# Feed-forward finish: the order of VectorE's maxima, scales and the second quarter's outputs

## The chip, the cores and the metric

The kernel runs on one core of one Trainium2 chip. The metric is the time of one execution in microseconds (us), as the device reports it. It was timed three times before the change: 2646.08, 2651.69 and 2651.78 us, median 2651.69 us.

The engines are named here as the profile names them: PE is TensorE, DVE is VectorE, ACT is ScalarE, POOL is GpSimd, SP is SyncE with the DMA queue. Each engine takes its instructions in program order; they meet only at semaphores.

## The reference

A decoder of six residual blocks for four batches of 1024 tokens of width 512. Only the last block is touched:

```python
x = _layernorm(x + _L1_xattn_ref(x, ctx_1024, ctx_1024), axis=-1)
x = _layernorm(x + _L1_ffn_ref(x, w1, conv_w, conv_b, w2), axis=-1)

def _L1_ffn_ref(...):                      # hidden width 2048
    h = bit_linear(x, w1)                  # quantised rows of x, ternary weights
    h = depthwise_conv1d(h)                # three taps along the tokens
    h = jax.nn.silu(h)
    return bit_linear(h, w2)

def act_quant(x):
    scale = 127.0 / jnp.clip(jnp.max(jnp.abs(x), axis=-1, keepdims=True), 1e-05)
    return jnp.clip(jnp.round(x * scale), -128, 127) / scale
```

So the second product needs, for every token, the largest absolute value over all 2048 hidden channels before any channel can be rounded. That maximum is what the change is about.

## The kernel before

`schedule(b)` writes out by hand, for each batch, one list of steps. Every engine walks the same list and does its own share of each step, so the list is the program order of all five engines at once.

The feed-forward takes the tokens of a batch in four quarters of 256 (`NSUB` is 4, s is 0 to 3; "the second quarter" is s = 1), and the hidden channels in 16 chunks of 128 (`M`), two chunks to a pair (k or i is 0 to 7). The steps, with the lines on which they show in the profile:

- `f_hidden(s, m)`: PE multiplies one chunk (L750). DVE takes it out of PSUM (f_g, L1357) and adds the last tap of the chunk two before (`last_tap`, L1089). ACT does the middle and first taps (L982, L984) and, with every second chunk, the SiLU of a pair (L808). POOL adds the first tap (L1418). `f_tail` is the rest of that pipeline after the last chunk: two taps on DVE, the SiLU of the last two pairs on ACT, two sums on POOL.
- `f_peak(s, k)`: PE transposes the pair (L759), DVE takes the maxima of it (f_top, L1367). At the last pair DVE goes on to the scales: five small operations (L1373 to L1377) and two diagonals (L1380).
- `f_scale(s)`: PE spreads the scales over the partitions (L765), ACT copies them to f_s2b (L992).
- `f_times(s, i)`: a pair of SiLU outputs times the scales (L374). POOL does it for all pairs of quarters 0 and 1 and pairs 0 to 4 of quarter 2; DVE does the rest.
- `f_quant(s, k)`: ACT rounds four chunks to f_hq (L1002).
- `f_part(s, t, k)`: PE multiplies four chunks by w2 into bank 6 or 7 (L778; before the first four a constant, L775). The first one of each output tile waits until the bank's previous output has been read.
- `f_out(s, t)`: DVE reads that bank and adds the residual (L1388), then two statistics (L1032, L1033); POOL makes the reciprocal deviation (rstd, L1405 and L1407).
- `f_norm(s, t)`: DVE normalises the tile (L1038), SP stores both tiles of a quarter.

Hidden chunks, `f_peak` and a few others share a ring of three PSUM banks (`dve_ring`): PE may claim the next bank only when DVE has emptied the one three claims before.

The twelve projections that open the next batch's attention (`a_key`, `a_query`, `a_value`) are spread among the chunks. The last of them is `a_key(3)`: eight records of matmul on PE (L386) and one copy on ACT (L839). The fourth batch has none.

The order after the last chunk comes from offsets: a step with offset n of quarter s stands behind chunk 16(s+1)+n of the 64, and whatever is past 63 stands after `f_tail`, in order of that number. The steps of the last quarter's maxima have offsets capped so that they come early. Before the change the list around the last chunk of a batch reads:

```
62: f_hidden(3,14) f_times(2,2) f_quant(2,0)
63: f_hidden(3,15) f_part(1,0,3) f_peak(3,3)
f_tail
64: f_out(1,0) f_part(1,1,3) f_times(2,3) a_key(3) of the next batch
65: f_out(1,1) f_peak(3,4) f_peak(3,5)
66: f_times(2,4) f_quant(2,1) f_peak(3,6) f_peak(3,7)
67: f_norm(1,0) f_part(2,0,0)
68: f_norm(1,1) f_times(2,5) f_part(2,1,0)
70: f_times(2,6) f_quant(2,2)
71: f_part(2,0,1)     72: f_times(2,7) f_part(2,1,1)
73: f_scale(3)        74: f_quant(2,3) f_times(3,0) to f_times(3,3)
```

and then the parts and outputs of quarters 2 and 3. The next batch's attention begins when they are done.

Of the kernel before, what the change touches and what calls it, by code (L numbers as in the profile page):

```python
# [30 lines left out]
M = F // P  # L31
# [42 lines left out]
def attends_until(i):  # L74
# [4 lines left out]
FIRST_PROJECTIONS = [("a_key", 0), ("a_query", 0), ("a_value", 0), ("a_key", 1), ("a_value", 1), ("a_query", 2),  # L79
                     ("a_value", 2), ("a_query", 1), ("a_value", 3), ("a_key", 2), ("a_query", 3), ("a_key", 3)]  # L80
# [72 lines left out]
def schedule(b):  # L153

    steps = (WARM_UP if b == 0 else []) + [("a_begin",), ("weight", 3)]
    for i in range(len(GROUPS) + 2):
        g, k = divmod(i, 5)
# [67 lines left out]
    at = {}  # L225
    for s in range(NSUB):
        last = s == NSUB - 1
        later = [(min(2 * k + 9 - M, k // 2 - 1) if last else 2 * k + 9 - M, ("f_peak", s, k)) for k in range(M // 2)]
        later += [(9 if last else 10, ("f_scale", s)),
                  (32, ("f_out", s, 0)), (33, ("f_out", s, 1)), (35, ("f_norm", s, 0)), (36, ("f_norm", s, 1))]  # L230
        later += [((10 if i < 4 else 18) if last else 10 + 2 * i, ("f_times", s, i)) for i in range(M // 2)]
        later += [(14 + 4 * k, ("f_quant", s, k)) for k in range(4)]
        later += [(19 + 4 * k + t, ("f_part", s, t, k)) for k in range(4) for t in range(2)]
        for offset, step in later:
            at.setdefault(M * (s + 1) + offset, []).append(step)
# [2 lines left out]
                    (10, ("f_unit", 1))):  # L238
        at.setdefault(n, []).append(step)
    if b < B - 1:  # L240
        for n, step in zip((2, 3, 5, 6, 14, 21, 28, 35, 42, 49, 56, 64), FIRST_PROJECTIONS):
            at.setdefault(n, []).append(("next", step))
    for n in range(NSUB * M):
        steps += [("f_hidden", *divmod(n, M))] + at.pop(n, [])
# [36 lines left out]
def sequence(nc, dram, sb, banks, sems):  # L281

    order = [step for b in range(B) for step in schedule(b)]
    q = sems
    now = [0]
# [1459 lines left out]
```

## Time and profile before

| | us |
|---|---|
| median of three runs (lowest, highest) | 2651.69 (2646.08, 2651.78) |
| the profiled execution's own time | 2647.19 |
| its span, first to last instruction | 2645.4 |
| PE busy (89% of the span) | 2362.2 |
| DVE busy (60%) | 1578.6 |
| ACT busy (47%) | 1243.5 |
| POOL busy (26%) | 687.5 |
| mean granted TensorE clock | 0.975 |

All times of the trace are read against the 2645.4 us span. Between span and time lie 1.8 us. The four batches are alike; the end of the third batch's feed-forward lies at about 1970 to 2003 us, that of the fourth at 2610 to 2642 us. The busy shares are averages over stages with different limits, so a change in the order of one stage is read from the timeline of that stage.

### The profile page before, as it was taken

To read this page: it belongs to the slowest core of one execution; us is meant where nothing else is said; L and a number is where in the kernel's file an instruction comes from. 1 tells how busy PE (TensorE), PEld (TensorE's weight loads), DVE (VectorE), ACT (ScalarE), POOL (GpSimd) and SP (SyncE) were. 2 spreads that over 40 slices of the span, in tenths; PEclk is the share of its full clock that TensorE was granted. 3 is DMA by queue.
4 is the path that set the end of the run, shared out by engine and by line. 5 is a ranking of instruction groups with operands and counts; after the bars stand their busy time and mean duration, and the time that the engine had idled before them with its cause. 6 is when DMAs were issued, how large, how long until landed. Compare 5 with 4: busy or idle time off the path is not lost.

```text
span 2645.4 us, 36993 instructions
## 1 busy us (share of the span) xinstructions
PE 2362.2 (89%) x12984; PEld 1312.7 (50%) x13000; DVE 1578.6 (60%) x3101; ACT 1243.5 (47%) x2858; POOL 687.5 (26%) x989
## 2 busy tenths in 40 slices
PE   7889999988888999998988999988898899999867
PEld 3655544445465544444546554444455655444444
DVE  4664634468776462557867655165786746516588
ACT  5753312268674422227857441222885733122396
POOL 0002321037301232013820213101480022310266
PEclk9999999999999999999999999999999999999888
DMA  8001101010300210000030110001003010100000
GB/s 296 17 10 51 49 16 32 0 48 6 112 18 10 71 29 16 32 16 33 9 126 2 45 36 28 32 16 48 1 9 126 2 57 23 37 8 1 0 1 32
DMA packets 58987, 99.41 MB, mean 38 GB/s; under 512 B 13364, under 2 KB 13748, under 8 KB 58296
## 3 DMA queue, kind: packets, MB, share of 16 engines
q1 hardware_dynamic: 58808, 97.06, 11.1%
q8 instruction: 108, 1.77, 0.3%
q14 instruction: 71, 0.58, 0.1%
HBM read 88.66 MB, written 8.39 MB: 37 GB/s over the span
## 4 chain that ended last, share of the span: by engine, by line
PE 65%; DVE 20%; ACT 9%; issue 5%; POOL 0%; DMA 0%; DVEq 0%; ACTq 0%; POOLq 0%; SPq 0%
PE psum L392 22%; PE psum L386 17%; DVE neg_max L1082 5%; PE psum L486 4%; PE psum L470 3%; PE psum L536 2%; DVE f_a L1089 2%; DVE turned L1132 2%; PE psum L778 2%; ACT xT L820 1%; PE psum L750 1%; DVE f_top L1367 1%; DVE f_g L1357 1%; PE psum L556 1%; DVE bn L1032 1%
## 5 line engine op out<-in xcount | busy, mean ns | idle before, releaser
L386 PE MATMUL psum<-xT,weights 128*128 128x512 f32 x1152 | 511.5, 597 | 16.7 <-DMA weights<-in_a_k 10.3
L386 PEld LDWEIGHTS psum<-xT,weights 128*128 128x128 f32 x1152 | 216.2, 192 | 267.3 <-issue 248.2
L392 PE MATMUL psum<-weights,mixed 128*128 128x512 f32 x768 | 339.0, 597 | 0.0
L797 ACT ACTIVATE prob<-psum,neg_max 128x128 f32<-128x128 f32 (+3 forms) x512 | 265.0, 543 | 104.5 <-DVE neg_max L1082 104.5
L392 PE MATMUL psum<-weights,xT 128*128 128x512 f32 x640 | 288.8, 595 | 2.4 <-DVE recip L1270 1.6
L1405 POOL TENSOR_SCALAR var<-stats 128x1 f32<-128x1 f32 x192 | 61.7, 321 | 789.6 <-DVE stats L1033 789.6
L1082 DVE TENSOR_REDUCE neg_max<-psum 128x1 f32<-128x128 f32 (+3 forms) x512 | 210.9, 481 | 67.5 <-PE psum L475 39.6
L486 PE MATMUL psum<-ident,prob 128*128 128x128 f32 x1280 | 172.2, 278 | 79.4 <-DVE turned L1132 72.4
L1418 POOL TENSOR_TENSOR f_a<-f_a,f_z 128x256 f32<-128x256 f32 x256 | 199.6, 789 | 133.7 <-DVE f_a L1089 127.1
L392 PEld LDWEIGHTS psum<-weights,mixed 128*128 128x128 f32 x768 | 144.5, 192 | 179.9 <-issue 179.2
L820 ACT COPY xT<-psum 128x512 f32<-128x512 f32 x128 | 67.1, 596 | 333.8 <-PE psum L423 333.8
L1063 DVE TENSOR_TENSOR x<-psum,x 128x512 f32<-128x512 f32 x128 | 88.3, 690 | 225.4 <-PE psum L392 163.4
L486 PEld LDWEIGHTS psum<-ident,prob 128*128 128x128 f32 x1280 | 141.9, 143 | 104.0 <-ACT prob L797 96.9
L392 PEld LDWEIGHTS psum<-weights,xT 128*128 128x128 f32 x640 | 117.5, 190 | 142.2 <-issue 141.9
L1089 DVE SCALAR_TENSOR_TENSOR f_a<-f_g,conv_w,f_a 128x256 f32<-128x256 f32 x256 | 170.9, 668 | 9.0 <-ACT f_a L982 8.6
L982 ACT ACTIVATE f_a<-f_g,conv_b,conv_w 128x256 f32<-128x256 f32 x256 | 152.8, 597 | 48.5 <-DVE f_g L1357 40.5
L750 PE MATMUL psum<-f_xqT,w 128*128 128x258 bf16 x1024 | 152.7, 280 | 25.2 <-DVE f_g L1357 21.7
L1132 DVE COPY turned<-psum 128x512 f32<-128x512 f32 x160 | 109.6, 685 | 92.6 <-PE psum L486 92.6
L1441 POOL COPY a_spread<-a_rcp 128x512 f32<-128x512 f32 x32 | 19.8, 617 | 539.1 <-DVE a_rcp L1137 539.1
L1357 DVE TENSOR_TENSOR f_g<-psum,f_unit 128x258 f32<-128x258 f32 x256 | 106.1, 416 | 70.1 <-PE psum L750 70.0
L1071 DVE SCALAR_TENSOR_TENSOR d_tot<-d_sum 128x4 f32<-128x4 f32 x16 | 2.6, 161 | 230.1 <-ACT d_kT L906 229.7
L750 PEld LDWEIGHTS psum<-f_xqT,w 128*128 128x128 fp8e4 x1024 | 97.8, 100 | 79.7 <-DVE f_g L1357 32.0
(243 smaller groups left out, 4052.3 us busy)
## 6 DMA issues: line engine op xcount, KB each, us to landing
xT<-in_xT SPq DMA_DIRECT2D x8, 1024.0 KB, 6.2
x<-in_x SPq DMA_DIRECT2D x8, 1024.0 KB, 7.9
out<-x SPq DMA_DIRECT2D x16, 512.0 KB, 2.8
weights<-in_a_k SPq DMA_DIRECT2D x4, 1024.0 KB, 5.2
weights<-in_a_q SPq DMA_DIRECT2D x4, 1024.0 KB, 5.0
weights<-in_a_v SPq DMA_DIRECT2D x4, 1024.0 KB, 5.0
w1f<-in_w SPq DMA_DIRECT2D x4, 1024.0 KB, 15.1
w2f<-in_w SPq DMA_DIRECT2D x4, 1024.0 KB, 17.3
```

Source lines behind the costliest of these rows:

```text
L386: last = mm(bank[:, 0:n], weights[weight][:, c, heads(g)], rhs(c), start=(c == 0), stop=(c == C - 1))
L392: last = mm(bank, lhsT(c), weights[weight][:, c, :], start=(c == 0), stop=(stop and c == C - 1))
L486: last = nc.tensor.transpose(bank[:, heads(k)], sb["prob"][:, (G * i + j) % PROB_SLOTS, heads(k)], ident[:])
L750: last = mm(bank[:, 0:SUB + 2], sb["w1"][:, c, heads(m)], sb["f_xqT"][:, c, SUB * s:SUB * s + SUB + 2], start=(c == 0), stop=(c == C - 1))
L797: last = run(sb["prob"][:, slot, o:o + keys], bank[:, o:o + keys], ACT.Exp, bias=sb["neg_max"][:, n, qc, j:j + 1], accum_out=sb["a_sum"][: ...
L820: copy(xT[:, :, heads(t)], bank.rearrange("p (c n) -> p c n", c=C)).then_inc(act_ring.freed, 1)
L982: run(sb["f_a"][:, i, :], g[:, 1:SUB + 1], ACT.Identity, scale=sb["conv_w"][:, m, 1:2], bias=sb["conv_b"][:, m:m + 1]).then_inc(q["f_tap_d ...
L1082: last = v.tensor_reduce(sb["neg_max"][:, n, qc, j:j + 1], bank[:, o:o + P * (qc + 1)], AX.X, ALU.max, negate=True)
L1089: v.scalar_tensor_tensor(sb["f_a"][:, i, :], sb["f_g"][:, i, 2:SUB + 2], sb["conv_w"][:, m, 2:3], sb["f_a"][:, i, :], ALU.mult, ALU.add).t ...
L1132: v.tensor_copy(dst, turn_ring.take(dve, step)[:, 0:dst.shape[1]]).then_inc(turn_ring.freed, 1)
L1357: v.tensor_tensor(sb["f_g"][:, n % DEPTH, :], bank[:, 0:SUB + 2], sb["f_unit"][:, SUB * s:SUB * s + SUB + 2], ALU.mult).then_inc(dve_ring. ...
L1418: g_.tensor_tensor(a, a, sb["f_z"][:, n % DEPTH, :], ALU.add).then_inc(q["f_conv_done"], 1)
```

## The change

Only `schedule` is changed. Three offsets move:

- `f_peak(3, 3)` goes from 63 to 62, `f_peak(3, 4)` and `f_peak(3, 5)` from 65 to 64; `f_peak(3, 6)` and `f_peak(3, 7)` stay at 66.
- `f_out(1, 0)` goes from 64 to 65, `f_out(1, 1)` from 65 to 67, behind the last maxima and the scales.
- The last projection of the next batch goes from 64 to 63, ahead of `f_tail`, and so ahead of `f_part(1, 1, 3)` and the last four `f_peak`.

```diff
-        later = [(min(2 * k + 9 - M, k // 2 - 1) if last else 2 * k + 9 - M, ("f_peak", s, k)) for k in range(M // 2)]
+        later = [(min(2 * k + 9 - M, 2 * (k // 2) - 4) if last else 2 * k + 9 - M, ("f_peak", s, k)) for k in range(M // 2)]
         later += [(9 if last else 10, ("f_scale", s)),
-                  (32, ("f_out", s, 0)), (33, ("f_out", s, 1)), (35, ("f_norm", s, 0)), (36, ("f_norm", s, 1))]
+                  (33 if s == 1 else 32, ("f_out", s, 0)), (35 if s == 1 else 33, ("f_out", s, 1)),
+                  (35, ("f_norm", s, 0)), (36, ("f_norm", s, 1))]
...
-        for n, step in zip((2, 3, 5, 6, 14, 21, 28, 35, 42, 49, 56, 64), FIRST_PROJECTIONS):
+        for n, step in zip((2, 3, 5, 6, 14, 21, 28, 35, 42, 49, 56, 63), FIRST_PROJECTIONS):
```

The list then reads:

```
62: f_hidden(3,14) f_times(2,2) f_quant(2,0) f_peak(3,3)
63: f_hidden(3,15) f_part(1,0,3) a_key(3) of the next batch
f_tail
64: f_part(1,1,3) f_times(2,3) f_peak(3,4) f_peak(3,5)
65: f_out(1,0)
66: f_times(2,4) f_quant(2,1) f_peak(3,6) f_peak(3,7)
67: f_out(1,1) f_norm(1,0) f_part(2,0,0)
68: f_norm(1,1) f_times(2,5) f_part(2,1,0)
```

with everything from 70 on as before. No instruction is added or taken away.

## Rows read from the trace of the kernel before

**Rows 1.** The page's part 4: shares of the chain that ended last.

```profile
PE 65%; DVE 20%; ACT 9%; issue 5%; POOL 0%; DMA 0%; DVEq 0%; ACTq 0%; POOLq 0%; SPq 0%
```

**Rows 2.** Chain in order of time, third batch's tail: start us, length us, what.

```profile
1980.22 0.71 PE psum L759 x4
...
1983.49 2.93 PE psum L778 x12
...
2003.18 0.76 DVE neg_max L1082 x2
```

**Rows 3.** Timeline, DVE, third tail: start, us, line, operation, out<-in, [idle before <-releaser].

```profile
1976.23 0.74 DVE L1388 SCALAR_TENSOR_TENSOR x<-psum,f_uh,x 128x512 f32<-128x512 f32 x1
...
1977.83 0.72 DVE L1388 SCALAR_TENSOR_TENSOR x<-psum,f_uh,x 128x512 f32<-128x512 f32 x1
...
1979.41 2.45 DVE L1367 TENSOR_REDUCE f_top<-psum 128x2 f32<-128x512 f32 x4
...
1983.54 0.99 DVE L1038 TENSOR_SCALAR x<-x,stats,rstd 128x512 f32<-128x512 f32 x2
1984.45 1.89 DVE L374 TENSOR_TENSOR f_y<-f_y,f_s2b 128x512 f32<-128x512 f32 x3
1987.29 2.50 DVE L374 TENSOR_TENSOR f_y<-f_y,f_s2b 128x512 f32<-128x512 f32 x4 [0.96 <-ACT f_s2b L992]
...
2002.72 0.55 DVE L1038 TENSOR_SCALAR x<-x,stats,rstd 128x512 f32<-128x512 f32 x1 [0.77 <-POOL rstd L1407]
```

**Rows 4.** Timeline, PE, the same stretch.

```profile
1971.12 0.63 PE L759 MATMUL psum<-ident,f_y 128*128 128x128 f32 x4
1971.59 1.03 PE L778 MATMUL psum<-w,f_hq 128*128 128x512 fp8e4 x4
1972.45 3.60 PE L386 MATMUL psum<-xT,weights 128*128 128x512 f32 x8
1975.88 1.04 PE L759 MATMUL psum<-ident,f_y 128*128 128x128 f32 x8
1977.62 0.65 PE L759 MATMUL psum<-ident,f_y 128*128 128x128 f32 x4 [0.70 <-ACT f_y L808]
...
1982.86 0.63 PE L775 MATMUL psum<-col_sum,off 128*128 128x512 f16 x1
...
1986.25 0.59 PE L765 MATMUL psum<-f_diag,ones 128*128 128x256 f32 x2
```

**Rows 5.** Timeline, ACT, the same stretch.

```profile
1967.35 1.13 ACT L1002 ACTIVATE f_hq<-f_y,offset_col 128x1024 f16<-128x1024 f32 x1
1968.39 0.35 ACT L992 COPY f_s2b<-psum 128x256 f32<-128x256 f32 x1
...
1985.22 1.15 ACT L1002 ACTIVATE f_hq<-f_y,offset_col 128x1024 f16<-128x1024 f32 x1 [3.70 <-DVE f_y L374]
1986.88 0.37 ACT L992 COPY f_s2b<-psum 128x256 f32<-128x256 f32 x1 [0.51 <-PE psum L765]
```

**Rows 6.** Busy time by stretch: us, busy of PE, PEld, DVE, ACT, POOL, clock, DMA.

```profile
1977.00:1979.00 2.00, 0.65 (x4) 0.42 (x4) 1.93 (x4) 1.26 (x3) 1.92 (x4) 1.00 0.00 0
...
1981.00:1983.00 2.00, 2.00 (x6) 0.73 (x5) 1.83 (x7) 0.52 (x1) 1.41 (x2) 0.50 0.03 8
```

**Rows 7.** Timeline of the fourth batch's tail, DVE and then PE.

```profile
2615.31 0.74 DVE L1388 SCALAR_TENSOR_TENSOR x<-psum,f_uh,x 128x512 f32<-128x512 f32 x1
...
2623.53 1.89 DVE L374 TENSOR_TENSOR f_y<-f_y,f_s2b 128x512 f32<-128x512 f32 x3
2626.17 2.50 DVE L374 TENSOR_TENSOR f_y<-f_y,f_s2b 128x512 f32<-128x512 f32 x4 [0.76 <-ACT f_s2b L992]
...
2615.25 0.91 PE L759 MATMUL psum<-ident,f_y 128*128 128x128 f32 x4 [2.88 <-ACT f_y L808]
...
2619.30 1.08 PE L759 MATMUL psum<-ident,f_y 128*128 128x128 f32 x4 [1.49 <-DVE f_top L1367]
...
2622.54 2.75 PE L778 MATMUL psum<-w,f_hq 128*128 128x512 fp8e4 x12
```

## The prediction

> **What bounds the kernel now.** I read the page first: the chain that ended last runs for 65% through PE and for 20% through DVE [rows 1], so most of the kernel is matmuls, and an order on DVE matters only where that chain leaves PE. Then I read the chain in order of time around the end of a batch's feed-forward. There it goes from the maxima into the last transposes, through the parts of quarter 2 on PE and on to the scales, and at 2003.18 it enters the maxima of the next batch's attention [rows 2]. So nothing covers this tail: a delay of the scales delays the rest of the batch, four times in the kernel. Last I read the three engines' timelines there [rows 3 to 5]. The reader is to see one thing: DVE works without a gap from the second quarter's first output at 1976.23 to the end of its first three products, which begin at 1984.45, and only then waits 0.96 us for the copied scales [rows 3]. ACT made that copy at 1986.88 after waiting 0.51 us for PE [rows 5], and PE had reached f_scale at 1986.25 behind the parts of quarter 2 [rows 4]. So the point to follow is the start of f_times(3, 0), at 1987.29 here and at 2626.17 in the fourth batch [rows 3, 7]. What comes behind it (four products, two outputs, the last quarter) is a chain on DVE, ACT and PE that only shifts with it.
>
> The scales are therefore ready too early already: DVE has the diagonals done at 1983.54 [rows 3], and PE does not come to them for 2.7 us. Making them still earlier is worth nothing by itself. What counts is when PE gets through f_part(2, 1, 0) to f_part(2, 1, 1), which stand ahead of f_scale, and when ACT gets through f_quant(2, 2), which stands ahead of the copy.
>
> **The parts of the change.** Nothing is added or removed, so all costs are waits.
>
> Step one, the earlier f_peak(3, 3). PE now does it before the last chunk, which needs the bank of f_peak(3, 2). That bank comes free where f_peak(3, 3) started, at 1971.12 [rows 4], so the last chunk starts at 1971.12 and DVE takes it one maximum (0.6 us) later than before. ACT reaches that chunk much later, behind a rounding of quarter 2. I cost this at nothing; if the cover were gone it would be 0.6 us.
>
> Step two, a_key(3) and the parts ahead of f_peak(3, 4). Before, f_peak(3, 4) was transposed at 1975.88, while DVE was to be busy with outputs until 1979.41, so it lay ready [rows 3, 4]. Now DVE wants it at 1976.23, the moment its last tap is done. PE goes from 1971.12 through the last chunk (0.44, as a group of four transposes from 1971.12 to 1971.59 about), two f_part (0.86 each: 1971.59 to 1972.45) and a_key(3) (3.43: 1972.45 to 1975.88) [rows 4]. That is 1971.12 + 0.44 + 1.72 + 3.43 = 1976.71. Four transposes take 0.65 us until they can be read, so DVE starts at 1977.37: a stall of 1.14 us, with the two outputs, which used to stand there, queued behind it. The copy of a_key(3) on ACT falls into a wait before the next SiLU; at nothing, or 0.5 us if it doesn't fit. In the fourth batch there is no projection: f_peak(3, 4) is ready, but f_peak(3, 5) is transposed at 2615.25 and takes 0.91 us [rows 7]. DVE is there at 2615.31 + 0.60, so it stalls 0.30 us, and f_peak(3, 7), 1.08 us long at that clock and behind the last SiLU, costs some 0.15 us more.
>
> Step three, f_out(1, 1) behind the scales. On DVE it takes 1.60 us (1976.23 to 1977.83) [rows 3], the same work in another place. But two things wait for it. First, f_part(2, 1, 0) needs its bank. DVE reaches it after the stall, four maxima and the scales (1979.41 to 1983.54 is 4.13 us) and one output (1.58): 1977.37 + 4.13 + 1.58 = 1983.1, and the bank is free 0.8 us later, at 1983.9. Before, PE was there at 1982.86 [rows 4]. PE is thus 1.1 us later with everything behind that part, f_scale among it. Secondly, f_norm(1, 0) and f_norm(1, 1) now follow it at once, while POOL must first make the rstd. The trace has this very pattern at a quarter's end: output, first normalisation, then 0.77 us of idle DVE for rstd [rows 3]. Before, there was none here. f_out(1, 0) has time enough. Bounds: 0.4 (the small POOL operations without a neighbour) and 0.8; I take 0.77.
>
> The sum for DVE: 1.14 + 0.77 = 1.91 us later at f_times(2, 5), so 1986.36 instead of 1984.45. ACT starts f_quant(2, 2) 0.77 us after it (1984.45 to 1985.22), and the copy of the scales 1.04 us after that (1967.35 to 1968.39) [rows 3, 5]: 1988.17. The product begins 0.41 us behind the start of the copy (1986.88 to 1987.29), at 1988.58. Against 1987.29 that is **+1.29 us**. The old wait for PE (0.51 us and a little of issue) takes up the rest of the 1.91. For the fourth batch the same working gives 0.30 + 0.15 + 0.77 = 1.22 us at 2623.53, so 2624.75, and 2626.97 for the product instead of 2626.17: **+0.8 us**. The sum without any change of the clock is 3 x 1.29 + 0.8 = **+4.7 us**.
>
> Step four, PE's clock. Before, PE had 0.65 us of work in the two microseconds from 1977 on, and soon after, from 1981 to 1983, the granted clock is 0.50, that is 1.2 instead of 2.4 GHz [rows 6]. Now PE does f_peak(3, 7) and f_part(2, 0, 0) by about 1980.5 and then stands still until 1983.9, longer than it did before. If the clock is at full rate, the parts from 1983.9 take 2.83 us (0.24 and 2.75 less the overlap of the last) [rows 7], f_scale starts at 1986.8 and ACT, at 1988.17, is the later: no cost. If the 3.4 us after the idle time are at half rate, 8 of the 13 matmuls take 0.43 instead of 0.22 us, 1.7 us more, f_scale starts at 1988.5, and the product at 1989.5: +2.2 us instead of +1.29. In the fourth batch the same gives +1.5. The sum is then 3 x 2.2 + 1.5 = **+8.1 us**. Which it is hangs on where in the idle time the clock falls. I take the middle, +6.4, as the slow stretch will often lie only partly on the parts.
>
> On this the Trainium skill has a page, TensorE: Matmul & The Clock Gate; its Part 1 (What's actually happening) says that the array is at half rate by default and that only activity lifts it, so that a TensorE left idle falls back. By that rule every tail pays and the sum would be the upper one, 8.1; the trace agrees as far as all tails show 0.50 after PE's pauses [rows 6], but it does not say how much of a pause here is enough.
>
> **Rivals.** (a) The gain that the order suggests. The scales are some 0.4 us earlier, f_quant(2, 1) and POOL's product too. If PE brings f_peak(3, 4) in time (no stall of 1.14) and keeps its full clock because its transposes are closer together, the copy of the scales no longer waits: at most the 0.51 to 0.6 us per tail goes, four times: -2.2 us. For it speaks that 0.50 of clock lay on just these parts before [rows 6]; against it that the projection's 3.43 us stand ahead of the transposes in any case [rows 4], and that the rstd wait remains. (b) The other side: slower beyond what can be told. Mechanism: after the idle time until 1983.9 PE stays at half rate for all 13 matmuls and f_scale. They then take 5.6 and 0.9 us, so the product starts at about 1990.8, +3.5 us, four times up to +13. It decides from a slow stretch of over 3.4 us on; the fourth tail's transposes at 2615.25 and 2619.30, both slow [rows 7], show that one can last so long. (c) The change does nothing that is seen: DVE's stalls are taken up by the old waits of 0.96 and 0.76 us [rows 3, 7], as they would if the stall on f_peak(3, 4) were half of what I work out: 0 to +2 us in all.
>
> **The numbers.** Against the profiled execution's 2647.19 us, the forecast is 2653.6 us. That execution lies low among the runs (median 2651.69, lowest 2646.08); on the median the same sum gives 2658.1. I take 2656 us, which lies between. A measurement of this kernel tells about 0.3% (8 us) from no change. Chances: forecast (+4 to +8.2) 0.57; (a) 0.08; (b) 0.15; (c) 0.17; something unseen that gains more, 0.03. The first case ends just under the limit, and a few hundredths of it lie past it. That gives faster 0.03, same 0.77, slower 0.20. For the range I leave out most of (a) and the upper half of (b): 2648 to 2663.
>
> **What would show it.** In the profile after: DVE idle of about 1.1 us before the maxima of f_peak(3, 4) with PE's L759 as the releaser, in three tails, and 0.3 us in the fourth; about 0.77 us before the second normalisation, released by POOL; f_part(2, 1, 0) at about 1 us later than before and released by DVE's x, L1388; a stretch of 0.50 on the parts of quarter 2. The batches' distance grows by 1.3 to 2.2 us. I am wrong if the maxima come at once after the last tap, if DVE's products of quarter 3 start sooner than before, or if the tails keep their length and the time moves elsewhere.

## The result and the profile after

| | before | changed |
|---|---|---|
| median of six runs | 2649.16 us (2646.08 to 2652.06) | 2663.1 us (2659.39 to 2663.53) |
| profiled execution, its span | 2647.19, 2645.4 us | 2663.33, 2661.5 us |
| PE busy | 2362.2 us | 2371.5 us |
| mean granted TensorE clock | 0.975 | 0.970 |

The changed kernel takes 1.0052 times as long (95% interval 1.0042 to 1.0062), about 14 us more. No instruction was added, and DVE, ACT and POOL have the busy times of before to 1.5 us. Two executions of the kernel before (4842.84 and 8169.13 us) and one of the run parts_first (8488.91 us) were slow as a whole and are in no ratio. The kernel has one line more, so L1368 here is L1367 of before, and so on.

The third batch's tail, first DVE (timeline: start us, length us, line, operation; in brackets the idle time before it and who ended it). It answers to [rows 3].

```profile
1986.25 0.98 DVE L1090 SCALAR_TENSOR_TENSOR f_a<-f_g,conv_w,f_a 128x256 f32<-128x256 f32 x1 [1.12 <-ACT f_a L983]
1988.20 1.29 DVE L1368 TENSOR_REDUCE f_top<-psum 128x2 f32<-128x512 f32 x2 [0.97 <-PE psum L760]
1989.41 0.74 DVE L1389 SCALAR_TENSOR_TENSOR x<-psum,f_uh,x 128x512 f32<-128x512 f32 x1
...
1991.02 1.25 DVE L1368 TENSOR_REDUCE f_top<-psum 128x2 f32<-128x512 f32 x2
1992.31 0.17 DVE L1374 TENSOR_REDUCE f_ah<-f_top 128x2 f32<-128x16 f32 x1
1992.51 0.80 DVE L1375 TENSOR_SCALAR f_ah<-f_ah 128x2 f32<-128x2 f32 x1
...
1994.41 0.74 DVE L1389 SCALAR_TENSOR_TENSOR x<-psum,f_uh,x 128x512 f32<-128x512 f32 x1
...
1997.29 0.55 DVE L1039 TENSOR_SCALAR x<-x,stats,rstd 128x512 f32<-128x512 f32 x1 [0.77 <-POOL rstd L1408]
1997.75 1.89 DVE L375 TENSOR_TENSOR f_y<-f_y,f_s2b 128x512 f32<-128x512 f32 x3
2000.53 2.50 DVE L375 TENSOR_TENSOR f_y<-f_y,f_s2b 128x512 f32<-128x512 f32 x4 [0.89 <-ACT f_s2b L993]
```

DVE now waits in two places where it did not before: 0.97 us for the transposes of f_peak(3,4), and 0.77 us for rstd. Then PE and ACT (timelines), which answer to [rows 4] and [rows 5]; L387 is the projection, L760 the transposes:

```profile
1983.27 3.60 PE L387 MATMUL psum<-xT,weights 128*128 128x512 f32 x8
1986.70 1.03 PE L779 MATMUL psum<-w,f_hq 128*128 128x512 fp8e4 x4
1987.57 1.62 PE L760 MATMUL psum<-ident,f_y 128*128 128x128 f32 x12
...
1990.61 1.03 PE L779 MATMUL psum<-w,f_hq 128*128 128x512 fp8e4 x4
1995.21 0.61 PE L776 MATMUL psum<-col_sum,off 128*128 128x512 f16 x1 [3.57 <-DVE x L1389]
1995.61 4.05 PE L779 MATMUL psum<-w,f_hq 128*128 128x512 fp8e4 x12
1999.49 0.59 PE L766 MATMUL psum<-f_diag,ones 128*128 128x256 f32 x2
...
1998.53 1.15 ACT L1003 ACTIVATE f_hq<-f_y,offset_col 128x1024 f16<-128x1024 f32 x1 [6.93 <-DVE f_y L375]
2000.13 0.37 ACT L993 COPY f_s2b<-psum 128x256 f32<-128x256 f32 x1 [0.45 <-PE psum L766]
```

PE stands still for 3.57 us until DVE has read the bank of f_out(1,1), and then needs 4.28 us from the first of the 13 matmuls to f_scale (1995.21 to 1999.49), where the fourth batch before needed under 3 [rows 7] and the third, already partly slow, 3.39 (1982.86 to 1986.25 [rows 4]). The busy time by stretch (us; PE, PEld, DVE, ACT, POOL; granted clock; DMA) says why; it answers to [rows 6]:

```profile
1992.00:1995.00 3.00, 0.00 (x0) 0.00 (x0) 2.79 (x9) 0.00 (x0) 1.28 (x2) 0.97 0.00 0
1995.00:1998.00 3.00, 2.79 (x7) 1.04 (x8) 2.17 (x6) 0.00 (x0) 0.99 (x2) 0.50 0.00 0
1998.00:2001.00 3.00, 3.00 (x14) 1.49 (x13) 2.11 (x4) 2.02 (x3) 0.00 (x0) 0.96 0.46 175
```

PE did nothing from 1992 to 1995, and from 1995 to 1998 the parts behind it ran at 0.50, that is 1.2 GHz.

**How much of it is the tail.** I measure a tail from the start of the last tap of chunk 63 (L1089 before; the first row of DVE above, 1986.25) to the first maxima of the next batch's attention. In the first three batches it was 27.85, 27.59 and 27.86 us and is now 30.18, 29.90 and 30.17, in the fourth (to the last normalisation) 27.29 and 29.11. That is 2.3 us in each of three and 1.8 in the last, 8.8 us in all. The two profiled spans differ by 16.1. The other 7.4 us lie in stages in which nothing was changed, ahead of the feed-forward of each batch: 4.2 us in the first batch, before the first changed step is run at all, and 1.0 to 1.1 us in each of the other three. From the first chunk of the feed-forward to the start of the tail nothing is lost. In the stages ahead of the feed-forward the granted clock differs. Summed over them, it was 0.50 for 13.7 us of the first batch and 23.9 us of each later one before, and for 23.9 and 27.3 us in the changed kernel. For the first batch, the first two rows are of before and the second two of the changed kernel, over the same microseconds (the columns as above); the changed kernel is 1.6 us behind at 430 and 3.2 us at 477, so its rows hold partly other instructions:

```profile
430.00:434.00 4.00, 4.00 (x21) 1.82 (x20) 3.96 (x2) 0.00 (x0) 0.00 (x0) 1.00 0.22 83
477.00:481.00 4.00, 3.93 (x24) 1.74 (x17) 2.73 (x5) 1.92 (x5) 0.00 (x0) 1.00 0.00 0
```

```profile
430.00:434.00 4.00, 3.74 (x36) 1.13 (x36) 2.74 (x4) 0.00 (x0) 0.00 (x0) 0.69 0.61 221
477.00:481.00 4.00, 2.76 (x24) 1.56 (x28) 1.43 (x5) 1.75 (x2) 0.00 (x0) 0.79 0.00 0
```

One group of sixteen matmuls, the same in both kernels, shows what the clock costs there (timelines of PE, before and then changed):

```profile
476.22 1.92 PE L404 MATMUL psum<-d_kT,d_thin 128*32 128x512 f32 x16
...
479.44 3.52 PE L405 MATMUL psum<-d_kT,d_thin 128*32 128x512 f32 x16
```

What happens in the first batch is a matter of the execution, not of the kernel. Three runs below differ from the kernel before only from the second batch on, and yet their first tails start at 678.16, 682.23 and 677.99 us (delay1, delay3, delay8), against 678.12 before and 682.33 in the changed kernel. The kernel before itself gave nearly all its times in two groups, about 2646 to 2647.5 and 2649 to 2652.5 us. Its profiled execution was of the lower group, so 16.1 us is more than the 14 of the medians. Without the first batch's share the two profiled executions differ by some 12 us: 8.8 in the tails and 3.2 in the later batches' stages ahead of the feed-forward.

### The profile page after: what moved, and what is told of

Same layout as the page of the kernel before. It is cut to its first block, busy times and chain, and to the rows that moved or that the text cites. A ratio compares the mean times of both kernels' runs of the same rounds, so it can differ in the third digit from the quotient of the medians.

```text
span 2661.5 us, 36993 instructions
## 1 busy us (share of the span) xinstructions
PE 2371.5 (89%) x12984; PEld 1314.6 (49%) x13000; DVE 1578.3 (59%) x3101; ACT 1242.2 (47%) x2858; POOL 687.8 (26%) x989
## 4 chain that ended last, share of the span: by engine, by line
PE 67%; DVE 20%; ACT 8%; issue 4%; POOL 0%; DMA 0%; DVEq 0%; ACTq 0%; POOLq 0%; SPq 0%
PE psum L393 22%; PE psum L387 18%; DVE neg_max L1083 5%; PE psum L487 4%; PE psum L471 3%; PE psum L779 2%; PE psum L537 2%; PE psum L751 2%; DVE turned L1133 2%; DVE f_top L1368 2%; ACT xT L821 1%; DVE f_a L1090 1%; DVE f_g L1358 1%; PE psum L557 1%; PE psum L608 1%
## 5 line engine op out<-in xcount | busy, mean ns | idle before, releaser
L387 PE MATMUL psum<-xT,weights 128*128 128x512 f32 x1152 | 509.6, 596 | 16.6 <-DMA weights<-in_a_k 10.2
L387 PEld LDWEIGHTS psum<-xT,weights 128*128 128x128 f32 x1152 | 215.1, 191 | 266.1 <-issue 247.1
L1090 DVE SCALAR_TENSOR_TENSOR f_a<-f_g,conv_w,f_a 128x256 f32<-128x256 f32 x256 | 167.5, 654 | 12.2 <-ACT f_a L983 11.7
## 6 DMA issues: line engine op xcount, KB each, us to landing
w1f<-in_w SPq DMA_DIRECT2D x4, 1024.0 KB, 14.8
```

Source lines behind the costliest of these rows:

```text
L387: last = mm(bank[:, 0:n], weights[weight][:, c, heads(g)], rhs(c), start=(c == 0), stop=(c == C - 1))
L1090: v.scalar_tensor_tensor(sb["f_a"][:, i, :], sb["f_g"][:, i, 2:SUB + 2], sb["conv_w"][:, m, 2:3], sb["f_a"][:, i, :], ALU.mult, ALU.add).t ...
```

## The experiments

Each kernel is timed against runs of the kernel before on the same chip. "Tail" is that of the third batch. "Distance" is the time from the first attention maxima of the second batch to those of the third, and from the third to the fourth. Both are of the one profiled execution (before: 27.86; 648.66 and 648.55). The last column gives that execution's time and the median of the kernel's runs. Where the two lie far apart, as in outs_only, no_key and parts_first, tail and distances stand for that execution and not for the ratio beside them.

| kernel | ratio to before (95%) | tail | distances | profiled (median) |
|---|---|---|---|---|
| changed | 1.0052 (1.0042 to 1.0062) | 30.17 | 651.97, 651.94 | 2663.33 (2663.10) |
| key_only | 0.9995 (0.9987 to 1.0004) | 27.86 | 648.60, 648.52 | 2646.67 (2646.89) |
| peaks_only | 1.0009 (0.9999 to 1.0019) | 29.19 | 645.67, 651.55 | 2652.41 (2654.95) |
| outs_only | 1.0036 (1.0024 to 1.0048) | 29.60 | 651.93, 651.97 | 2663.41 (2658.81) |
| no_key | 1.0021 (1.0012 to 1.0030) | 32.24 | 648.84, 651.53 | 2663.86 (2655.95) |
| out_early | 1.0021 (1.0011 to 1.0031) | 30.41 | 648.40, 648.53 | 2652.17 (2653.98) |
| norms_late | 1.0024 (1.0013 to 1.0035) | 30.33 | 652.10, 648.36 | 2658.16 (2656.13) |
| delay1 | 1.0000 (0.9989 to 1.0012) | 28.52 | 648.83, 648.58 | 2643.99 (2648.21) |
| delay3 | 1.0044 (1.0032 to 1.0056) | 29.83 | 651.90, 651.97 | 2661.29 (2661.29) |
| delay8 | 1.0094 (1.0081 to 1.0107) | 33.14 | 655.58, 655.35 | 2670.10 (2674.74) |
| scale_norms | 1.0005 (0.9996 to 1.0014) | 27.65 | 648.55, 648.56 | 2646.91 (2650.68) |
| parts_first | 0.9988 (0.9977 to 0.9999) | 28.90 | 651.97, 651.99 | 2652.37 (2646.70) |
| parts_scale_norms | 1.0015 (1.0006 to 1.0025) | 28.58 | 651.68, 648.79 | 2657.79 (2655.43) |

### The parts of the change one at a time

**key_only.** The kernel before with one line of the change:

```diff
-        for n, step in zip((2, 3, 5, 6, 14, 21, 28, 35, 42, 49, 56, 64), FIRST_PROJECTIONS):
+        for n, step in zip((2, 3, 5, 6, 14, 21, 28, 35, 42, 49, 56, 63), FIRST_PROJECTIONS):
```

> Only the last projection moves from 64 to 63; maxima and outputs stand as before. Theory A (the cost is DVE's and PE's waits in the tail, added up): the maxima are not wanted until DVE is through with two outputs, so nothing waits for the projection; the distance between two batches stays at 648.5 us and the total within 1 us. Theory B (a small delay of the tail moves the stretches in which TensorE has 1.2 GHz, and these cost more than the delay): no delay here, so 0 as well, 648.5 us from batch to batch. Theory C (the projection's place alone is the cost): about +14 us in total.

Tail and distances are those of before to a tenth. The projection's place costs nothing while the maxima stand behind the outputs. Theory C of this run falls; A and B both gave what was found.

**peaks_only.** Only the line with the offsets of f_peak.

```diff
-        later = [(min(2 * k + 9 - M, k // 2 - 1) if last else 2 * k + 9 - M, ("f_peak", s, k)) for k in range(M // 2)]
+        later = [(min(2 * k + 9 - M, 2 * (k // 2) - 4) if last else 2 * k + 9 - M, ("f_peak", s, k)) for k in range(M // 2)]
```

> Only the offsets of f_peak(3,3) to f_peak(3,5) move; the projection stays behind them and the outputs stand as before. Theory A: the order on DVE becomes output, two maxima, output, two maxima; the projection (3.4 us of PE) now lies ahead of f_peak(3,6), which is about 0.1 us late: +0.1 to +0.4 us a tail, +0.5 to +1.5 in total. Theory B: under about half a microsecond a tail the batches keep their 648.5 us; past it they jump to about 652 us and the total to +13.

The tail grew by 1.3 us, not by the 0.1 to 0.4 of theory A: DVE waits 1.85 us for f_peak(3,6), which stands behind the projection, and the projection ran partly at 1.2 GHz (first row DVE's timeline, second the busy time by stretch):

```profile
1987.65 1.29 DVE L1367 TENSOR_REDUCE f_top<-psum 128x2 f32<-128x512 f32 x2 [1.85 <-PE psum L759]
...
1982.00:1985.00 3.00, 3.00 (x6) 1.19 (x5) 2.90 (x7) 1.26 (x2) 2.92 (x5) 0.55 0.02 5
```

The four tails are 1.3, 1.6, 1.3 and 0.2 us longer, 4.5 us in all; the ratio gives 2.4 us (-0.3 to +5.0), so that it is not told from 0. Theory B, a jump to about 652 us a batch and +13 in total once a tail grows by more than half a microsecond, is wrong here: the distances are 645.67 and 651.55, and +13 lies far outside.

**outs_only.** Only the offsets of the two outputs.

```diff
-                  (32, ("f_out", s, 0)), (33, ("f_out", s, 1)), (35, ("f_norm", s, 0)), (36, ("f_norm", s, 1))]
+                  (33 if s == 1 else 32, ("f_out", s, 0)), (35 if s == 1 else 33, ("f_out", s, 1)),
+                  (35, ("f_norm", s, 0)), (36, ("f_norm", s, 1))]
```

> Only f_out(1,0) and f_out(1,1) move. Theory A: no stall before the maxima, but the 0.77 us wait for rstd before f_norm(1,1) is there; DVE is 0.77 us later at f_times(2,5) and the product by the scales about 0.15 us later: +0.6 us in total. Theory B: the same if the batches stay at 648.5 us, +13 us if even this moves the slow stretches; a number between these two speaks against B.

This part alone makes most of the change: +1.74 us of tail, distances of 652.0 as in the changed kernel, and 1.0036, whose interval overlaps that of the whole change. Of the 1.74 us, 0.6 is the later bank (f_part(2,1,0) 8.17 us after the last tap, 7.54 before) and 1.1 the slower clock (4.50 us from there to f_scale, 3.39 before). Theory A's 0.15 us a tail was too little. The distances are those that B gave, but the total is +9.5 us (6.4 to 12.7), and a number between A's 0.6 and B's 13 was to speak against B: neither theory gives this total.

**no_key.** Both of these without the projection's line (the diff is against the changed kernel).

```diff
-        for n, step in zip((2, 3, 5, 6, 14, 21, 28, 35, 42, 49, 56, 63), FIRST_PROJECTIONS):
+        for n, step in zip((2, 3, 5, 6, 14, 21, 28, 35, 42, 49, 56, 64), FIRST_PROJECTIONS):
```

> The whole change but for the projection, which stays at 64 and so comes behind f_peak(3,5). Theory A: f_peak(3,4) is ready when DVE wants it (the 1.0 us stall is gone), but f_peak(3,6) stands behind the projection, ready at about 4.6 us after DVE's first maximum, a stall of about 1.6 us in three tails: +1.5 us a tail, +5 to +6 in total, like the whole change by its waits. Theory B: about 652 us from batch to batch and +13 us in total, as the whole change.

DVE waits 3.27 us for f_peak(3,6), twice what I expected:

```profile
1990.62 1.29 DVE L1367 TENSOR_REDUCE f_top<-psum 128x2 f32<-128x512 f32 x2 [3.27 <-PE psum L759]
```

The tail is the longest of all without a delay, 32.24 us, and yet the kernel is at 1.0021, below the changed one at 1.0052, and the intervals don't meet. So the projection does belong ahead of the maxima as far as the tail is concerned, and the tail 2 us longer than the changed kernel's did not make the kernel slower than that one. Theory A's total of +5 to +6 us is the measured 5.6 by luck: its tails were to be 1.5 us longer, and they are 4.4 to 4.7 us longer in three batches and 1.9 in the last in the profiled execution. That execution took 2663.86 us, as long as the changed kernel's, and was the second slowest of twelve; ten took 2651 to 2660. No tail of the quicker ones is on record, so it is not shown where they save their time.

### Which wait sets the tail

**norms_late.** The changed kernel with the rstd wait taken away.

```diff
-                  (35, ("f_norm", s, 0)), (36, ("f_norm", s, 1))]
+                  (41 if s == 1 else 35, ("f_norm", s, 0)), (41 if s == 1 else 36, ("f_norm", s, 1))]
```

> The changed kernel with f_norm(1,0) and f_norm(1,1) moved from 67 and 68 to 73, behind DVE's products of quarter 2: the wait of 0.77 us for rstd ahead of f_times(2,5) is gone. Theory A (the prediction's step: DVE's lateness at f_times(2,5) sets the copy of the scales): the product starts 0.7 us or more sooner in the tail, the tail is 1.5 us instead of 2.3 us longer than before. Theory B (PE sets it: it waits for the bank until the output behind the scales is read, and then runs the parts at 1.2 GHz): f_times(2,5) 1.7 us sooner, the copy of the scales at most 0.3 us sooner, and the total within 2 us of the changed kernel's.

The products of quarter 2 start 1.7 us sooner after the last tap (9.76 instead of 11.50 us), the wait of 0.77 us is gone, and the copy of the scales comes no sooner (14.03, against 13.87). It waits for PE (DVE, PE and ACT):

```profile
1990.46 1.86 DVE L374 TENSOR_TENSOR f_y<-f_y,f_s2b 128x512 f32<-128x512 f32 x3
...
1989.66 0.61 PE L775 MATMUL psum<-col_sum,off 128*128 128x512 f16 x1 [3.56 <-DVE x L1388]
1990.06 4.20 PE L778 MATMUL psum<-w,f_hq 128*128 128x512 fp8e4 x12
...
1994.73 0.37 ACT L992 COPY f_s2b<-psum 128x256 f32<-128x256 f32 x1 [2.36 <-PE psum L765]
```

For the tail that is theory B: PE's wait for the bank and its slow clock set it, and the two waits of DVE are covered. B's last number missed: the total was 7 us under the changed kernel's at the same tail. One of the two distances is 648.4 here and not 652; ahead of that batch's feed-forward the clock was 0.50 for 17.1 us instead of 27.3.

**out_early.** The changed kernel with f_out(1,1) ahead of the scales.

```diff
-                  (33 if s == 1 else 32, ("f_out", s, 0)), (35 if s == 1 else 33, ("f_out", s, 1)),
+                  (33 if s == 1 else 32, ("f_out", s, 0)), (34 if s == 1 else 33, ("f_out", s, 1)),
```

> The changed kernel, but f_out(1,1) one place earlier, so that it stands ahead of f_peak(3,6) and the scales. This takes away PE's wait for the bank (3.6 us of idle PE in the changed kernel) and the 0.77 us wait for rstd, and keeps the 1.0 us stall before the maxima of f_peak(3,4). Theory A (waits): the tail is 0.3 to 0.9 us longer than before the change instead of 2.3, total +1.5 to +4 us. Theory B (the slow clock on the parts after PE's idle time is what makes the output's place so dear): the same sign, and no 1.2 GHz stretch lies on the parts of quarter 2 any longer; total near the kernel before, within 3 us. Theory C (the stall before the maxima is the main cost): the tail stays over 1.5 us longer than before and the total about +8.

The bank is free at once, f_part(2,1,0) starts behind f_part(2,0,0) and runs at full clock; the copy of the scales comes 1.4 us sooner than in the changed kernel (12.50 us after the last tap). Then PE waits for the rounding, and now those parts run slowly, 5.10 us for 16 matmuls that took 3.62 before (PE's timeline, then busy time by stretch):

```profile
1985.50 0.39 PE L775 MATMUL psum<-col_sum,off 128*128 128x512 f16 x1
1985.73 2.75 PE L778 MATMUL psum<-w,f_hq 128*128 128x512 fp8e4 x12
1989.85 0.70 PE L765 MATMUL psum<-f_diag,ones 128*128 128x256 f32 x2 [1.37 <-DVE f_diag L1380]
1992.61 5.10 PE L778 MATMUL psum<-w,f_hq 128*128 128x512 fp8e4 x16 [2.06 <-ACT f_hq L1002]
...
1992.00:1995.00 3.00, 2.40 (x6) 0.87 (x7) 2.67 (x5) 2.64 (x4) 0.00 (x0) 0.54 0.34 128
```

The gain is given back within 5 us: the tail stays 2.55 us longer than before. Of that, 0.94 us is there at the copy of the scales, as much as the stall of 0.97 us before the maxima, which this run keeps; 1.6 us comes behind the scales, where the parts run slowly. Theory A's waits were right up to the scales and wrong for the tail. B was wrong in that a slow stretch does lie on the parts of quarter 2. C's sign, a tail over 1.5 us longer, is there, but the stall makes only the smaller part of it. The total, +5.6 us (2.9 to 8.2), decides nothing: it lies between A's upper end of 4 and C's 8, and above B's 3. It is less than the change, with distances of 648.4 and 648.5 although the tail is as long as the changed one.

### The same lateness without the change

Clears of an unused tile on DVE at the start of the second to the fourth batch (1 to 3 in the expectations, which count from 0), in the kernel before. No order is changed, and every stage of a batch is as it was. (In the expectations stages A to E are those ahead of the feed-forward.)

```diff
                         dve.wait_ge(q["f_out_filled"], at("f_out_filled", 0))
+                        for _ in range(3):
+                            link(v.memset(sb["recip"][:], 0.0))
```

(`range(1)` for delay1, `range(8)` for delay8.)

> The kernel before with one clear (0.66 us with its wait) at the start of batches 1 to 3. Theory A (waits only add): +2.0 us. Theory B (later stages move against the slow stretches): if 0.66 us is still taken up, as waits that were there get shorter, the batches stay at 648.5 us and the total at about 0 to +2; if not, they are at 652 us and the total is +13, as with three clears.

> The kernel before with three clears of an unused tile (128x512) on DVE at the start of batches 1 to 3, each waited for; nothing else is changed, and they lie on the chain, behind the last normalisation and ahead of the first maxima. They add some 1 to 1.8 us to each of three batches. Theory A (waits only add): three times their length as the profile shows it, +3 to +5 us. Theory B (the position of later stages against the slow stretches matters): each of the three batches becomes longer by some 3.4 us, total about +10 us, though stages A to E have no new instruction.

> The same with eight clears, some 2.5 to 4.5 us on each of three batches. Theory A: three times their length, +8 to +13 us, and clearly (5 us or more) above the run with three clears. Theory B: the batches' distance is again about 652 us if the added time is under 3.4 us, so the total is the same as with three clears to within 2 us; above that it jumps once more.

Each clear takes 0.66 us of the chain, so 1.98 us with three. DVE's timeline in delay3:

```profile
2013.51 0.55 DVE L1038 TENSOR_SCALAR x<-x,stats,rstd 128x512 f32<-128x512 f32 x1 [0.77 <-POOL rstd L1409]
2014.11 0.48 DVE L1098 MEMSET recip<- 128x512 f32 x1
2014.76 0.48 DVE L1098 MEMSET recip<- 128x512 f32 x1 [0.17 <-DVE recip L1098]
2015.42 0.48 DVE L1098 MEMSET recip<- 128x512 f32 x1 [0.17 <-PE psum L386]
2015.94 2.74 DVE L1082 TENSOR_REDUCE neg_max<-psum 128x1 f32<-128x128 f32 x8
```

| | inserted in all | measured (ratio times 2649) |
|---|---|---|
| delay1 | 2.0 us | 0 us (-2.9 to +3.2) |
| delay3 | 5.9 us | +11.7 us (+8.5 to +14.8) |
| delay8 | 15.8 us | +24.9 us (+21.5 to +28.3) |

Delay doesn't simply add. Two microseconds can't be told from none, six cost about twelve (8.5 at the least), and the distances are 648.7, 651.9 and 655.5 us for 0.66, 1.98 and 5.3 us inserted in a batch. delay3 has the changed kernel's distances to 0.1 us and nearly its total, with the tail's inside untouched. A part of its total is the first batch, in which nothing was inserted: of the 14.1 us between the profiled executions 4.1 lie there, which leaves 10.0 for the 5.9 inserted. In delay8 the first batch took its time of before, and the profiled executions differ by 22.9 us for the 15.8 inserted. delay3 and delay8 bear out theory B and not A; delay1 allows both.

### Three attempts at a better order

**scale_norms.** The kernel before; f_scale(3) and the norms of quarter 1 move.

```diff
-        later += [(9 if last else 10, ("f_scale", s)),
-                  (32, ("f_out", s, 0)), (33, ("f_out", s, 1)), (35, ("f_norm", s, 0)), (36, ("f_norm", s, 1))]
+        later += [(5 if last else 10, ("f_scale", s)),
+                  (32, ("f_out", s, 0)), (33, ("f_out", s, 1)), (43 if s == 1 else 35, ("f_norm", s, 0)), (43 if s == 1 else 36, ("f_norm", s, 1))]
```

> The kernel before with two other moves: f_scale(3) from 73 to 69, ahead of most parts of quarter 2, and f_norm(1,0) and f_norm(1,1) from 67 and 68 to 75, behind DVE's products by the new scales. Theory A: DVE's products of quarter 2 start 0.9 us sooner, the copied scales no longer wait for PE, the 0.96 us of idle DVE is used: the tail becomes 0.5 to 1.5 us shorter in each batch, total -2 to -6 us. Theory B: a tail that is shorter moves the slow stretches again; the total may be anything from -10 to +5. If the tail doesn't get shorter, the chain is bound by the parts on PE and not by the scales.

The copy of the scales comes 1.7 us sooner (9.84 us after the last tap), the tail is 0.2 us shorter: PE's parts bound it, as the last sentence of the expectation has it. No difference in time (1.0005, 0.9996 to 1.0014): theory A's -2 to -6 us is wrong.

**parts_first.** The kernel before; two parts of quarter 2 go into PE's pause.

```diff
-        later += [(19 + 4 * k + t, ("f_part", s, t, k)) for k in range(4) for t in range(2)]
+        later += [(18 if s == 2 and k == 0 else 19 + 4 * k + t, ("f_part", s, t, k)) for k in range(4) for t in range(2)]
```

> The kernel before with only f_part(2,0,0) and f_part(2,1,0) moved to 66, ahead of the last two maxima, where PE stood idle for 1.9 us. Theory A: PE reaches f_scale 1 to 2 us sooner, but DVE's products of quarter 2 and the rounding behind them now set the copy: the product by the scales starts 0.5 us sooner, the total -2 us. Theory B: besides, PE has no longer a pause that long, so the 1.2 GHz stretch on the parts of quarter 2 goes, and the tail gets 0.5 to 1.5 us shorter; the total anything from -14 (if the batches get shorter as a whole) to 0.

The copy comes 0.6 us sooner, but PE, through with its work early, pauses for 2.06 us before the rest of quarter 2 and then runs 16 matmuls in 5.31 us:

```profile
1990.42 0.70 PE L765 MATMUL psum<-f_diag,ones 128*128 128x256 f32 x2 [0.20 <-DVE f_diag L1380]
1993.17 5.31 PE L778 MATMUL psum<-w,f_hq 128*128 128x512 fp8e4 x16 [2.06 <-ACT f_hq L1002]
```

The granted clock was 0.71 from 1993 to 1996. The tail got 1.0 us longer, against both theories; the ratio of 0.9988 (0.9977 to 0.9999) is nonetheless the lowest of the study, and theory A's -2 us lies in its interval (-6.1 to -0.3). It is the only version that may beat both kernels, by a tenth of a per cent, with its interval's end all but at one. Its profiled execution was the slowest of the eleven counted (median 2646.70), so the distances of 652 us in the table are not those of most of its runs.

**parts_scale_norms.** Both together (the two diffs above).

> The last with f_scale(3) at 69 and the norms of quarter 1 at 75 as well. Theory A: DVE goes from the diagonals straight to its products of quarter 2 and on to those of quarter 3 without a wait: the product by the scales 1.5 to 1.9 us sooner, the tail 1 to 1.8 us shorter, the total -4 to -7 us. Theory B: the same in the tail, but the batches' distance falls to about 645 us and the total by 10 to 14 us, or it stays at 648.5 us and nearly all of the gain is given back in later stages.

The scales' copy came 2.1 us sooner, but the tail is 0.7 us longer and the kernel slower (1.0015, 1.0006 to 1.0025); both theories had a tail 1 to 1.8 us shorter. Again PE idled, 2.83 us ahead of f_scale, and went on slowly (PE's timeline, then busy time by stretch with a granted clock of 0.59):

```profile
1991.37 1.08 PE L765 MATMUL psum<-f_diag,ones 128*128 128x256 f32 x2 [2.83 <-DVE f_diag L1380]
1992.25 6.69 PE L778 MATMUL psum<-w,f_hq 128*128 128x512 fp8e4 x24
...
1991.00:1994.00 3.00, 2.63 (x7) 1.15 (x8) 3.00 (x7) 1.51 (x3) 0.00 (x0) 0.59 0.00 0
```

## Why the prediction was right or wrong

**What bounds the tail: right.** The tail is on the chain and everything up to the next batch's maxima shifts with it: from the product by the scales to the first maxima it is 15.89 us in the changed kernel (2000.53 to 2016.42) and 15.89 before (1987.29 to 2003.18).

**Step one: right.** The earlier f_peak(3,3) costs nothing: from the last tap of chunk 60 to that of chunk 63 it is 4.10 us before and 4.10 changed, and ACT still ends DVE's wait before the last tap (1.12 us, ACT f_a).

**Step two: right in kind and size.** 1.14 us were worked out for the stall before the maxima of f_peak(3,4), 0.97 measured, released by PE's transposes; in the fourth batch 0.30 and 0.37:

```profile
2630.68 0.69 DVE L1368 TENSOR_REDUCE f_top<-psum 128x2 f32<-128x512 f32 x1 [0.37 <-PE psum L760]
```

(The prediction's own terms for the fourth batch, 2615.25 + 0.91 against 2615.31 + 0.60, give 0.25 and not 0.30; the 0.15 us that it added there for f_peak(3,7) did not come.) key_only and no_key show that it takes both moves: with either alone there is no such stall at f_peak(3,4).

**Step three: the waits right, what they set wrong.** The rstd wait is 0.77 us as read from [rows 3], and PE gets the bank 3.57 us after its last part, where 3.4 was worked out. Not in the sum was 0.46 us of DVE: the second of the small scale operations takes 0.80 us instead of 0.34, see below. So f_times(2,5) is 2.4 us later after the last tap (11.50 instead of 9.12), not 1.91; 0.97, 0.77 and 0.46 make 2.2 of that. But what failed is the next statement, that f_quant(2,2) on ACT then sets the copy while PE is covered: ACT waited 0.45 us for PE, and with DVE's lateness taken away (norms_late) the copy stayed where it was. It is PE that sets it, as only the upper case of step four had it: +2.3 us a tail instead of +1.29.

**Step four, the clock: right, and in the upper part.** 4.28 instead of 2.83 us for the parts, 1.4 us, where 1.7 was the bound; the tails came to 2.3 us each (2.2 for the case of a slow stretch wholly on the parts) and 1.8 in the fourth (1.5). The middle value I took was not what came: in the trace the clock fell at 1994.81 and rose at 1998.22, so 3.0 of its 3.4 us lay on the parts. The sum of the upper case, 8.1 us, is near the 8.8 us of the four tails. In part that is luck: f_part(2,1,0) started 8.95 us after the last tap, where the prediction's numbers give 8.6, and the slow stretch cost less than its bound, so two errors of 0.3 to 0.4 us cancel.

**The total: wrong by the rest.** The forecast was 2656 us and +6.4; measured were 2663.1 and +14 (11 to 16 by the interval), past the 0.3% that I gave 0.20, and at the very top of the range. The step that failed is the last one, from the tails to the time: it put everything outside the tails at nothing. It isn't nothing. The batches' distance grew by 3.3 to 3.4 us, not by the 1.3 to 2.2 forecast, with a tail 2.3 us longer, while the stages ahead of each feed-forward, in which no instruction was changed, spent 27.3 instead of 23.9 us at 1.2 GHz. delay3 shows it without the change: 5.9 us inserted, 11.7 us measured. That the time lies at the range's end at all is luck. The top of the range came from half of rival (b), and (b) had the right sign and about the right size for the wrong reason: it put up to 3.5 us on each tail, with PE at half rate through all 13 matmuls and f_scale. The slow stretch ended before that (f_scale is at 0.96 in the rows above), a tail cost 2.3, and the rest was paid in other stages. In (a) and (c) the old waits or an earlier maximum would have covered the lateness; the rows above refute both.

**What stays open.** Why the distances take values near 648.5, 652 and 655.5 in most kernels and not those between, and why no_key, norms_late and out_early, with tails as long as the changed kernel's or longer, come out 7 to 8 us lower. It is shown that batches spend different times at 1.2 GHz ahead of the feed-forward (27.3 us in each later batch of the changed kernel, 17.1 in out_early, 13.7 to 30.7 in no_key, each in one execution), and that a plain delay does the same (30.7 in delay3). No run controlled where a slow stretch begins, so that it is the cause of all that lies outside the tails is the best reading and not proven.

## What to carry to other kernels

A step put off on one engine must be followed through the banks and semaphores it frees: f_out(1,1) cost DVE nothing and stopped PE for 3.57 us. Where PE has pauses, the sum of the waits bounded the total in neither direction here: time saved ahead of the scales was paid back three times by slow matmuls behind them (out_early, parts_first, parts_scale_norms), 6 us of plain delay cost 12, and 4.5 us of longer tails could not be told from none (peaks_only). Read a small change in such a kernel by the length of the stretch that it touches, and take the total for what it is only after a plain delay of the same size has been timed beside it.

## What the runs showed of the hardware

**A delay isn't linear.** 0.66, 1.98 and 5.3 us inserted in each of three batches cost 0, 12 and 25 us in all (2, 5.9 and 15.8 inserted; 8.5 and 21.5 are the lower ends of the last two), with nothing else changed; in delay3 a part of it lies in the first batch, as said there.

**A small DVE operation waits for POOL.** The clip of f_ah (two elements a partition, SBUF to SBUF) takes 0.17 us alone, as in peaks_only and no_key, where POOL has no product at that moment; it takes 0.34 in the third tail before, 0.80 in the changed kernel's and 0.98 in that of outs_only. In the changed kernel it ends when POOL's product does (DVE's row stands above, 1992.51 + 0.80 = 1993.31; POOL's is this, 1992.02 + 1.26 = 1993.28):

```profile
1992.02 1.26 POOL L375 TENSOR_TENSOR f_y<-f_y,f_s2b 128x512 f32<-128x512 f32 x1
```

Before, too, both ended together (1982.44 and 1982.42), as these rows show; POOL's product had begun 0.95 us ahead of it there, and 0.49 us ahead of it here. It moved because f_out(1,0), and with it the rstd ahead of that product, moved.

```profile
1982.10 0.34 DVE L1374 TENSOR_SCALAR f_ah<-f_ah 128x2 f32<-128x2 f32 x1
...
1981.15 1.27 POOL L374 TENSOR_TENSOR f_y<-f_y,f_s2b 128x512 f32<-128x512 f32 x1
```

Not every DVE operation waits: the reduction just ahead of the clip took its 0.17 us in the middle of POOL's product (1992.31 in the changed kernel). The Trainium skill says on SBUF — State Buffer (SBUF: two separate sides) that DVE in a two-port mode and GpSimd take a shared pair of ports as a lock for a whole instruction; by that rule, if the clip runs in such a mode, the wait is what is left of POOL's product. The trace agrees in the length of the wait; in which mode the clip runs it doesn't show.
